# Moving the bucket copy-out behind two low-part subtractions in VectorE's step of a graph-network edge stage

## The reference

```
def mlp(x, W0, b0, W1, b1, g, b):
    h = silu(x @ W0 + b0)
    return layernorm(h @ W1 + b1) * g + b
e     = mlp(edge_attr_4, emb_...)                      # 21250 x 512
e_in  = concat([e, mesh_nfeat[src], x[dst]])
e_new = mlp(e_in, edge_...) + e
agg   = segment_sum(e_new, dst, 1250)
n_new = mlp(concat([x, agg]), node_...) + x
out   = layernorm(x + n_new)
```

## Time and profile before

| | |
|---|---|
| median of 3 runs | 2417.75 us (2416.12 to 2422.61) |
| the profiled execution | 2417.75 us, span 2416.0 us |
| busy share PE / PEld / DVE / ACT / POOL | 92 / 78 / 61 / 50 / 46 % |
| mean granted TensorE clock | 0.972 |

### The profile page before, as it was taken

The page is one execution under the profiler, slowest core; times in us unless marked ns, Lnnn a source line. Parts: engine busy times, 40 slices in busy tenths (PEclk is TensorE's granted clock), DMA queues, the critical chain, the costliest instruction groups (busy, mean ns, idle before and its releaser), DMA issues. The chain is left out here.

```text
span 2416.0 us, 44677 instructions
## 1 busy us (share of the span) xinstructions
PE 2222.8 (92%) x13057; PEld 1886.8 (78%) x13060; DVE 1475.7 (61%) x3258; ACT 1217.5 (50%) x2255; POOL 1120.9 (46%) x1665
## 2 busy tenths in 40 slices
PE   2989499999987799999999999999999999999797
PEld 1436388777765698898989988898898989889676
DVE  7012299534362567766677677766767677766566
ACT  0121111324321667666776766766767766667421
POOL 4777700000000455655556556555555556555323
PEclk9999799999998899999999999999999999999899
DMA  6223100000022532332323332332233333223121
GB/s 192 80 48 88 12 8 0 36 5 35 26 88 97 156 64 61 65 64 59 63 61 65 65 61 62 64 65 61 61 65 61 65 61 66 60 61 64 25 92 43
DMA packets 76276, 149.66 MB, mean 62 GB/s; under 512 B 14689, under 2 KB 15789, under 8 KB 76219
## 3 DMA queue, kind: packets, MB, share of 16 engines
q0 software_dynamic: 44864, 93.18, 19.7%
q1 hardware_dynamic: 31243, 55.63, 6.9%
q10 hardware_dynamic: 112, 0.11, 0.0%
HBM read 129.12 MB, written 19.46 MB: 61 GB/s over the span
## 5 line engine op out<-in xcount | busy, mean ns | idle before, releaser
L1180 POOL DMA_INDIRECT c_from_src<-s_dst_table,c_at_nodes x176 | 298.0, 1693 | 32.1 <-issue 32.1
L1529 PE MATMUL c_edge_bank<-c_m_hi,c_pt_hi 128*128 128x512 f32 x704 | 294.2, 418 | 0.0
L1303 DVE CUSTOM_DVE_ANT_0 c_var_bank<-c_var_bank,c_p,k_floor 128x512 f32<-128x512 f32 x176 | 132.4, 752 | 250.9 <-PE c_var_bank L1474 250.0
L1530 PE MATMUL c_edge_bank<-c_m_lo,c_pt_hi 128*128 128x512 f32 x704 | 279.6, 397 | 0.0
L1531 PE MATMUL c_edge_bank<-c_m_hi,c_pt_lo 128*128 128x512 f32 x704 | 278.4, 395 | 0.0
L1174 POOL DMA_INDIRECT c_from_src<-s_mesh_table,c_at_nodes x176 | 202.1, 1148 | 152.1 <-POOL c_at_nodes L1170 142.8
L1186 POOL TENSOR_TENSOR c_dev<-c_var,k_half 128x1 f32<-128x1 f32 x176 | 97.8, 556 | 319.2 <-DVE c_var L1287 319.2
L1417 ACT ACTIVATE c_h<-c_from_src 128x512 f32<-128x512 f32 x176 | 111.3, 633 | 265.2 <-DVE c_from_src L1322 265.2
L321 POOL DMA_INDIRECT s_records<-a_stage_rec,a_stage_row x170 | 207.6, 1221 | 56.8 <-issue 48.8
L1472 PE MATMUL c_var_bank<-c_m_hi,c_pt_hi 128*128 128x384 f32 x704 | 224.8, 319 | 7.8 <-ACT c_var_bank L1391 5.3
L1472 PE MATMUL c_var_bank<-c_m_hi,c_ht_hi 128*128 128x384 f32 x704 | 221.5, 315 | 4.9 <-DVE c_ht_lo L1292 4.6
(11 more groups left out here) (314 smaller groups left out, 5981.5 us busy)
## 6 DMA issues: line engine op xcount, KB each, us to landing
k_w<-in_L_gnn_Ws_self_dram SPq DMA_DIRECT2D x3, 1024.0 KB, 10.7
k_w<-in_L_gnn_Ws_neigh_dram SPq DMA_DIRECT2D x3, 1024.0 KB, 13.1
c_from_src<-s_mesh_table,c_at_nodes POOLq DMA_INDIRECT x176, 3.5
c_from_src<-s_dst_table,c_at_nodes POOLq DMA_INDIRECT x176, 4.7
s_records<-a_stage_rec,a_stage_row POOLq DMA_INDIRECT x170, 2.6
a_mesh<-in_L_gnn_mesh_nfeat_dram SPq DMA_DIRECT2D x10, 250.0 KB
k_h<-in_x_dram SPq DMA_DIRECT2D x1, 2500.0 KB
s_mesh_table<-a_mesh_out SPq DMA_DIRECT2D x10, 250.0 KB
```

What stands on the lines that cost most here:

```text
L1180: pool.indirect_dma_start(from_src[u][:], None, scratch["dst_table"], bass.IndirectOffsetOnAxis(ap=at_nodes[u][:, 1:2], axis=0), compute_o ...
L1303: dve.tensor_tensor_reduce(var1_bank[:], var1_bank[:], p[u % 2][:], 1.0 / D, k["floor"][:, 0:1], ALU.mult, ALU.add, var[u][:, 0:1]).then_i ...
L1529: pe.matmul(edge_bank[:], left[0], m_hi[1][:, c, :], start=False, stop=False, skip_group_check=True)
L1530: pe.matmul(edge_bank[:], left[0], m_lo[1][:, c, :], start=False, stop=False, skip_group_check=True)
```

## The change

Two edits in VectorE's `step`. `leave(n - 3)` stood at the step's start, right behind `add_r(n - 3)` and ahead of the first variance; now it stands behind `low_ht(n - 1)` and ahead of `low_rh(n - 2)`. And `low_p(n + 1)` stood ahead of `low_ht` in odd steps and behind it in even ones; now it is ahead of it in all. The tail of the phase behind the loop, in which the tenth bucket is copied out, is as it was.

```
@@ -1296,7 +1296,6 @@
             n = GROUP * i + u
             if exists(n - 3):
                 add_r(n - 3)
-                leave(n - 3)
 
             dve.wait_ge(var1_mm, n + 1)
             dve.wait_ge(p_ok, n + 1)
@@ -1304,12 +1303,12 @@
                                      ALU.mult, ALU.add, var[u][:, 0:1]).then_inc(var1_ok, 1)
             dve.wait_ge(var1_ok, n + 1)
             dve.tensor_scalar(var[u][:, 2:3], var[u][:, 0:1], EPS, None, ALU.max).then_inc(bound1_ok, 1)
-            if u % 2 and exists(n + 1):
+            if exists(n + 1):
                 low_p(n + 1, (u + 1) % 4)
             if exists(n - 1):
                 low_ht(n - 1, (u - 1) % 4)
-            if u % 2 == 0:
-                low_p(n + 1, u + 1)
+            if exists(n - 3):
+                leave(n - 3)
             if exists(n - 2):
                 low_rh(n - 2, (u - 2) % 4)
```

## The result

The changed kernel takes 2430.73 us (median of 12 runs, 2425.73 to 2436.17) against 2417.88 us (12 runs, 2415.99 to 2422.61). The ratio is 1.0056, 95% interval 1.0048 to 1.0063: slower by 12.85 us, where +7.1 was forecast. This median lies at the top of the range of 2417.5 to 2431; over all 29 executions of the changed kernel on record it is 2432.24, above the range. The spread of the runs has grown too, from 6.6 to 10.4 us.

What follows compares the result with a forecast made beforehand. TensorE was taken to bound the edge stage. Nine copies at 2.0 us less 0.1 make 17.9 us lost against 10.8 now, +7.1 on 2417.75: 2424.9, said as 2425; 8-in-10 range 2417.5 to 2431.

Steps and rivals of the forecast that it cites:

- The bound: Edge stage, 176 tiles: TensorE's, busy 497.39 of 500.00 us; VectorE's order only changes TensorE's idle time, 13.1 us lost.
- the loads in the 167 other steps: VectorE's register load and branch in steps without a copy, between `low_ht` and `low_rh`: hidden, cost 0.
- The direction and the mechanism: Copy steps: TensorE's stall moves from `variance2` (for `low_ht`) to `sums` and is longer; +7.1 us in all.
- the deadline of the hot matrix: Hot matrix must end 0.87 us before the sums, at V + 4.16; 0.73 us of room for a 2.53 us body.
- TensorE loses 1.90 + 0.10 of restart = 2.0 us per copy.: Nine copy steps: sums start at V + 6.93 instead of V + 5.03, plus 0.10 restart; u = 1 some 0.1 less.
- 0.87 to the sums.: `sums`: TensorE reads and tests the bucket number after the hot matrix, so its sums start 0.87 us after that ends.
- TensorE's clock falls ... Chance 0.05.: Rival, slower: the nine new idle gaps lower TensorE's clock, 1.7 us each, 15 in all, 2440; chance 0.05.
- The later losses go too: Rival, no change: 2.3 us lost in steps without a copy also vanish, +4.8, 2422.5; chance 0.14 with a shorter wait.
- No second stall taken: Behind the late `low_rh`, z and `turn_h` come about 2.5 us late, but a whole square product covers it: no cost.

Runs made afterwards that it cites:

- experiment 1: Kernel before with the copy-out alone moved behind the two low-part subtractions, their order unchanged; 2434.84 us, ratio 1.0077.
- 3: Changed kernel with TensorE's register load of the bucket number ahead of its waits in `sums`; 2420.71 us against 2416.66 before.
- 4: Changed kernel with the hot matrix made ahead of the copy-out and the sums waiting for `rh_lo` only at their third matmul; 2416.84 us, ratio 1.0004.
- the filled wait, 6: Changed kernel with ten matmuls of zeros on TensorE between `variance2` and the sums, in copy steps only; 2428.53 us, ratio 1.0050.
- experiment 9: Kernel before with VectorE's load ahead of `variance2`, body behind `add_r` at step's end, and TensorE's load ahead of its waits; 2405.83 us, ratio 0.9948.
- experiment 5: Changed kernel with one more copy of a bank, into a spare tile, in the body of `leave`; 2436.12 us, ratio 1.0080.
- experiment 2: Kernel before with `low_p` ahead of `low_ht` in every step and nothing else; 2421.35 us, ratio 1.0018.
- 8: Kernel before with VectorE's bucket-end load ahead of `variance2`, `add_r` and body behind it at the step's end; 2409.63 us, ratio 0.9967.
- 11: Kernel before with both register loads ahead and `low_ht` ahead of `low_p` in all steps; 2403.49 us, ratio 0.9943, and 2404.60 us when repeated.

## Where the prediction went wrong, and what of it was right

*The bound.* Right: what moved the time is TensorE's idle time and its clock, and nothing else. Four tiles stay at 33.07 and the loads in the 167 other steps cost nothing that shows.

*The direction and the mechanism.* Right: the wait for `low_ht` vanished, a longer one at the sums came, by the deadline of the hot matrix. Experiments 1 (the move carries it) and 3 (the load behind the hot matrix is a part of each) show it.

*"TensorE loses 1.90 + 0.10 of restart = 2.0 us per copy."* Right where TensorE's load takes 0.31: 1.9 to 2.0 at u = 1 and 2. VectorE's times were right to 0.1, but for u = 1, where the body came 0.2 later.

*"0.87 to the sums."* Mis-sized in six steps of nine. It was read from a step in which the load ran at another moment; here it took 0.60 to 0.86 us instead of 0.31. Nine copy waits so cost 9 x 1.92 + 6 x 0.33 = 19.3 us instead of 17.9.

*"TensorE's clock falls ... Chance 0.05."* This is the step that failed: the sum put the clock at nothing. The rival was all or nothing, nine falls or none, and had one chance in twenty. What happens is three of nine in both profiles of this kernel, at 1.57 us each, 4.7 us. From one window of 1.89 us of idle time that kept its clock I concluded for all; there was another such stretch in the same trace (at 647 us), and two are no sample of something that comes one time in three. It also goes with the spread of the runs: of the 29 executions on record the seven at a granted clock of 0.968 took 2432.3 to 2436.2 us, and the two at 0.972 took 2425.7 and 2427.0. 19.3 + 4.7 = 24.0 against 10.7 in the copy steps, +13.3, and the other steps lose 0.4 less: +12.9 in the stage. The measured +12.85 is a median of runs that spread over 10 us, and the profiled pair differs by 14.6, so the close agreement is in part luck.

*"The later losses go too."* No: 2.0 us of the 2.3 stayed.

*"No second stall taken."* Right for this kernel, as it seems only because TensorE was late itself: z and h come 1.4 to 2.3 us late (2.5 forecast). Experiments 3 and 4 show the losses that stood behind it, outside the copy intervals 3 us more than before in one and nearly 8 us more in the other.

What stays open: what slows TensorE's register load in six copy steps; what decides which of the long waits is followed by a fall of the clock; why the filled wait, which keeps the clock up, gains only 2.3 of its 4.7 us as a median.

## What to carry to other kernels

A rare body (one step in eighteen here) costs what its place in the step costs, so ask at each place for the next deadline: of the places tried here, the one in front of the first variance, where VectorE idles for TensorE, is the best. Take the register load that decides about it out of the chain first, on the engine that runs it and on the one that waits behind it; the two loads alone were worth 12 us (experiment 9). And where a wait on TensorE nears two microseconds, put a term for the clock into the sum as a share of the cases, 15 of 36 here, not as a rival that is or isn't.

## What the runs showed of the hardware

- A wait of TensorE of 1.5 to 2.3 us inside dense work was followed by half the clock in 15 of 36 cases (3 and 3 of nine in the two profiles of the changed kernel, 5 in experiment 1, 4 in experiment 5), and in experiment 2 in two of the three copy steps at u = 0, after waits of 1.9 us. The fifteen are among the 28 waits of 1.72 us and more. Each cost 1.5 to 1.6 us. Waits of up to 1.2 us (before, and experiments 3, 4, 6 and 8 to 11) were never followed by one in this stage.
- The register load of TensorE took 0.30 us in the median and 0.60 to 0.86 in six of 174 cases of the changed kernel. A full DMA share does not explain them: 1.07 around a load of 0.65 us, 1.06 around one of 0.30 in experiment 5.
- VectorE's sequencer executed a register load 0.2 us before the instruction ahead of it in the program had started (965.8 against 966.04 in the changed kernel).
